# Image attention written as one stream of steps, with the expert weights split by GpSimd under it and the blank rows filled from GpSimd's queue in the token block

## The reference

```
# 1. image attention (L0)
hn = group_norm(x, 32 groups) * gamma + beta
q, k, v = conv1x1(hn, wq, bq), conv1x1(hn, wk, bk), conv1x1(hn, wv, bv)      # [b, 256, 1024]
attn = softmax(q^T k / sqrt(256), over keys)                                # [b, 1024, 1024]
x = x + conv1x1(v attn^T, wp, bp)
# 2. token block (L1_attn), t = tokens of x
u = layernorm(t);  h = rms_norm(u) * norm1_w
q, k = hyperbolic_linear(0.5 h onto the ball, q_w / k_w);  v = h v_w^T      # 8 heads of 32
a = softmax(-|q - k|^2 / sqrt(32), causal) v
y = u + a o_w^T;  h2 = rms_norm(y) * norm2_w
t = t + y + (silu(h2 gate_w^T) * (h2 up_w^T)) down_w^T
# 3. experts (L1_ffn): 8 experts, the top 2 for each token, hidden size 1024
t = t + sum_e comb[:, e] * (gelu(ln(t) w1[e]^T + b1[e]) w2[e]^T + b2[e])
```

## Time and profile before

| | |
|---|---|
| median of 3 runs | 1593.93 us (1593.6 to 1602.22) |
| profiled execution | 1580.31 us, of which the span is 1578.5 |
| busy: PE, DVE, ACT, POOL | 1219.1, 773.9, 708.9, 462.5 us |
| image attention | 26.9 to 336.2 us, PE busy for 246.0 |
| hand-over and first loads of the token block | 336.2 to 353.5 us, PE busy for 3.9 |
| token block up to its first scores | 353.5 to 420.4 us, PE busy for 27.3 |
| rest of the token block | 420.4 to 985 us, PE busy for 469.3 |
| routing, experts, output | 985 to 1578.5 us, PE busy for 465.7 |

### The profile page before, as it was taken

The page is one execution under the profiler, slowest core; times in us unless marked ns, Lnnn a source line. Parts: engine busy times, 40 slices in busy tenths (PEclk is TensorE's granted clock), DMA queues, the critical chain, the costliest instruction groups (busy, mean ns, idle before and its releaser), DMA issues. The chain is left out here.

```text
span 1578.5 us, 27016 instructions
## 1 busy us (share of the span) xinstructions
PE 1219.1 (77%) x8981; PEld 780.2 (49%) x8982; DVE 773.9 (49%) x1444; ACT 708.9 (45%) x1330; POOL 462.5 (29%) x403
## 2 busy tenths in 40 slices
PE   3888979546398789768977988532499999999992
PEld 1443434223134433333444334431388888888882
DVE  3855463405556564755466544643144444444441
ACT  3554352316566766766775663321133233333321
POOL 0000000010393059107800860177132233322331
PEclk9989999868699989998998999555799999999996
DMA  4486795950642084119403620999433333333326
GB/s 133 120 214 174 188 234 152 281 170 16 117 145 87 15 187 137 39 41 189 147 1 70 170 83 25 243 263 228 77 48 48 52 53 48 49 50 53 51 33 222
DMA packets 347541, 183.49 MB, mean 116 GB/s; under 512 B 271040, under 2 KB 333760, under 8 KB 347328
## 3 DMA queue, kind: packets, MB, share of 16 engines
q1 hardware_dynamic: 313920, 124.66, 34.2%
q0 software_dynamic: 25184, 56.64, 14.6%
q10 hardware_dynamic: 8352, 1.08, 0.5%
HBM read 38.66 MB, written 83.11 MB: 77 GB/s over the span
## 5 line engine op out<-in xcount | busy, mean ns | idle before, releaser
L2077 ACT ACTIVATE moe_hid<-moe_hbank,moe_b1T 128x256 f32<-128x256 f32 x312 | 130.4, 471 | 265.3 <-PE moe_hbank L2034 265.3
L2034 PE MATMUL moe_hbank<-moe_xT,l_w1T 128*128 128x256 f16 x1872 | 212.2, 274 | 42.9 <-DMA moe_xT<-rows_scratch 41.8
L2034 PEld LDWEIGHTS moe_hbank<-moe_xT,l_w1T 128*128 x1872 | 183.7, 98 | 65.2 <-issue 43.4
L2013 POOL DMA_INDIRECT acc_scratch<-moe_y,moe_meta x78 | 122.1, 1565 | 310.7 <-DVE moe_y L2104 288.1
L2049 PE MATMUL moe_ybank<-l_w2T,moe_hid_hi 128*128 x1248 | 206.4, 273 | 0.1
L1109 ACT ACTIVATE block_probs<-block_bank 128x1024 f32<-128x1024 f32 (+1 forms) x192 | 144.8, 809 | 76.6 <-PE block_bank L853 62.8
L2049 PE MATMUL moe_ybank<-l_w2T,moe_hid_lo 128*128 x624 | 170.1, 273 | 0.0
L2089 DVE TENSOR_SCALAR moe_hid_hi<-moe_hid 128x2048 f16<-128x2048 f32 x39 | 47.8, 1227 | 207.0 <-ACT moe_hid L2077 207.0
L2049 PEld LDWEIGHTS moe_ybank<-l_w2T,moe_hid_hi 128*128 128x128 f16 x1248 | 122.1, 98 | 14.6 <-issue 0.4
L850 PE MATMUL block_bank<-block_qkT 128*128 128x512 f16 (+3 forms) x384 | 95.9, 339 | 39.9 <-DMA block_qkT<-block_stack 28.8
L700 POOL COPY block_stack<-block_stack 128x512 f16<-128x512 f16 x16 | 11.2, 700 | 317.6 <-ACT block_stack L1093 317.6
(11 more groups left out here) (330 smaller groups left out, 2490.1 us busy)
## 6 DMA issues: line engine op xcount, KB each, us to landing
rows_scratch<-l_blank SPq DMA_DIRECT2D x32, 1056.0 KB, 5.7
block_raw<-in_L_ffn_w POOLq DMA_DIRECT2D x32, 512.0 KB, 4.6
w_parts<-block_raw_hi POOLq DMA_DIRECT2D x32, 256.0 KB, 4.4
w_parts<-block_raw_lo POOLq DMA_DIRECT2D x32, 256.0 KB, 4.7
l_xs<-in_x SPq DMA_DIRECT2D x8, 512.0 KB, 7.3
x_scratch<-l_xs SPq DMA_DIRECT2D x4, 1024.0 KB, 4.0
block_xin<-x_scratch SPq DMA_DIRECT2D x16, 256.0 KB, 4.4
acc_scratch<-block_res SPq DMA_DIRECT2D x16, 256.0 KB, 2.2
```

Of the source, the lines that this page charges most:

```text
L2013: pool.indirect_dma_start(acc, bass.IndirectOffsetOnAxis(ap=meta[r][:, t, 0:1].bitcast(U32), axis=0), y[r % 2][:, t, :], None, compute_op= ...
L2034: last = pe.matmul(hbank[:, c, :], w1T[:, e, wp, k, c * P:(c + 1) * P], xT[q][:, xp * CC + k, :], start=n == 0, stop=n == 5)
L2077: act.activation(hid[q][:, c, :], hbank[:, c, :], ACT.Gelu, bias=b1T[:, e, c:c + 1], scale=1.0 / (GAIN * GAIN)).then_inc(S["gelu_done"], 1)
```

## The change

The image attention becomes one list of 32 steps (`STEPS`), one for each tile of 128 queries. In step n TensorE makes the scores of tile n, then the weighted sum of tile n - 3 (`weighted`, `LAG` = 3), and then the share of the next image's 12 projection units that falls to this step: all 12 of image 1 in step 7, one or two in each step of images 1 and 2 (`share`). Queries, not channels, are now the output rows of the weighted sum: each has 24 matmuls 256 wide into one half of the bank `avx`. Two fp32 transposes put the tile's x into its other half. The probabilities are no longer divided by their row sum before they are split (scale `P_GAIN` instead of `rowinv`); `mix` does that on the output. `q` and `k` get two buffers each, the projections lose two of their four banks. SyncE stores half images as tokens.

GpSimd gets a list in this block: for each image two additions of `fold_bias` to `xs`, and 6, 6, 6 and 14 pieces of the expert weights. The block ends for GpSimd when all parts are stored.

The token block loads `t1` directly from `x1`, which now is [tokens x channels]; `x_turned`, `x_copy`, `xin` and their waits are gone. GpSimd's list there has the 34 fills, nine behind the four copies of each of the first three images and seven behind those of the last.

```diff
...
+                for n in range(STEPS):
+                    q = n % SLOTS
+                    if n >= SLOTS:
+                        sp.wait_ge(av_full, n - SLOTS + 1)
+                    sp.wait_ge(ph_hi_done, n + 1)
+                    sp.dma_start_transpose(pt_hi[q][:, :, :], ph_hi[q][:, :]).then_inc(turned[q], 16)
+                    sp.wait_ge(ph_lo_done, n + 1)
+                    sp.dma_start_transpose(pt_lo[q][:, :, :], ph_lo[q][:, :]).then_inc(turned[q], 16)
+                    if n >= 2 * HALF and n % HALF == 0:
+                        store(n // HALF - 2)
...
-                        for dst, src in fills[n::STEPS]:
-                            sp.dma_start(dst, src).then_inc(filled, 16)
...
+                def weighted(n):
+
+                    b, i, q = n // QB, n % QB, n % SLOTS
+                    if i == 0:
+                        pe.wait_ge(x_biased, CC * (b + 1))
+                        pe.wait_ge(unit_done, UNITS * (b + 1))
...
+                    if n >= 2:
+                        pe.wait_ge(mixed_done, n - 1)
...
+                    for c in range(CC):
+                        pe.transpose(avx[n % 2][:, 1, c * P:(c + 1) * P], xs[:, b, c, i * P:(i + 1) * P], ident[:, :])
+                    pe.wait_ge(turned[q], 32 * (n // SLOTS + 1))
+                    split_product(pe, avx[n % 2][:, 0, :], [(pt_hi[q][:, j, :], pt_lo[q][:, j, :], v_hi[b % 2][:, j, :], v_lo[b % 2][:, j, :])
+                                                            for j in range(QB)]).then_inc(av_full, 1)
...
+                    scores(b, i)
+                    if n >= LAG:
+                        weighted(n - LAG)
...
+                    for u in share(b, i):
+                        if u == 0:
+                            pe.wait_ge(hn_ready, (b + 2) * CC)
+                        unit(b + 1, u)
...
+            @block.gpsimd
...
+                load_piece(0)
+                load_piece(1)
                 for b in range(B):
...
+                    for c in range(CC):
+                        pool.wait_ge(hn_act, 2 * (b * CC + c) + 1)
+                        pool.tensor_scalar(xs[:, b, c, :], xs[:, b, c, :], fold_bias[:, c:c + 1], None, ALU.add).then_inc(x_biased, 1)
+                    for n in pieces_of(b):
+                        split_piece(n)
+                for q in range(2):
+                    pool.wait_ge(parts_stored[q], 16 * len(splits))
...
+                for n in range(STEPS):
+                    b, i = n // QB, n % QB
+                    row_max(b, i)
...
+                    if n >= LAG:
+                        weights_lo(n)
+                        inverse(n)
+                        residual(n - LAG)
...
+                for n, (dst, blank_row) in enumerate(fills):
+                    if n % (len(fills) // B + 1) == 0:
+                        second_high(n // (len(fills) // B + 1))
+                    pool.dma_start(dst, blank_row).then_inc(filled, 16)
+                pool.wait_ge(filled, 16 * len(fills))
...
                 def load(b, pr):
-                    if not isinstance(b, int) or b or pr > 1:
-                        sp.wait_ge(S["x_full"], b * PAIRS + (pr - 1))
-                    sp.dma_start(xin[pr % 2][:, :, :], x1[b].rearrange("(c p) (n q) -> n p c q", p=P, q=2 * P)[pr]).then_inc(S[f"xin{pr % 2}"], 16)
+                    sp.wait_ge(S["res_done"], b * PAIRS)
+                    sp.dma_start(t1[:, 2 * pr:2 * pr + 2, :], x1.rearrange("b (n t p) d -> b n p t d", p=P, t=2)[b, pr]).then_inc(S[f"x_loaded{pr}"], 16)
...
```

More of the change, by code:

```diff
@@ L279, with conv_attention @@
 PIECE = 1024
-def conv_attention(nc, xs, x1, scale, shift, norm, fills, w, bias, bias_loaded, fold_bias):
+def conv_attention(nc, xs, x1, scale, shift, norm, splits, raw_loaded, parts_stored, w, bias, bias_loaded, fold_bias, ident):
     SCALE = float(C) ** -0.5 / CW_GAIN ** 2
-    QKV, AV = 12, 4
+    UNITS, LAG = 12, 3
     SLOTS = 4
+    STEPS = B * QB
+    HALF = QB // 2
     with ExitStack() as ctx:
@@ L336, in _ @@
+                store(2 * B - 2)
+                store(2 * B - 1)
+                for half in stored:
+                    sp.wait_ge(half, 16 * B)
             @block.tensor
             def _(pe):
[L338 to L347, removed]
@@ new lines, in _ @@
+                pe.wait_ge(hn_ready, CC)
+                for u in range(UNITS):
+                    unit(0, u)
+                for n in range(STEPS):
[3 more added lines that the diff above has]
+                        weighted(n - LAG)
+                    if n == 2:
+                        pe.wait_ge(unit_done, UNITS)
+                        norm.average(pe, averages)
+                    for u in share(b, i):
+                        if u == 0:
+                            pe.wait_ge(hn_ready, (b + 2) * CC)
+                        unit(b + 1, u)
@@ L408, in _ @@
+                for n in range(STEPS - LAG, STEPS):
+                    weighted(n)
             @block.scalar
@@ new lines, in _ @@
+                for n in range(STEPS):
+                    b, i = n // QB, n % QB
+                    exps(b, i)
+                    if n >= LAG:
+                        mix(n - LAG)
+                    if n == 4:
+                        norm.root(act)
+                    if n == 5:
+                        act.wait_ge(norm.ready, 1)
+                        normalise(1)
+                    if n == 6:
+                        normalise(2)
+                    for u in share(b, i):
+                        high_part(b + 1, u)
+                    if n == QB + 2:
+                        normalise(3)
@@ L571, with token_block @@
 BARRIER = 4096.0
-def token_block(nc, x1, t2, ident, ident_h, weights, norm1_w, norm2_w, splits):
+def token_block(nc, x1, t2, ident, ident_h, weights, norm1_w, norm2_w, fills, filled):
     SCALE = 2.0 / (float(HD) ** 0.5 * QK_GAIN ** 2)
@@ L955, in first_front @@
                 def first_front():
-                    for pr in range(PAIRS):
-                        x_turned(0, pr)
                     for n in range(QKV_STRIPS):
@@ L2208, in build @@
         s = Scope(nc, whole, "all")
+        filled = s.sem("filled")
+        raw_loaded, parts_stored = ([s.sem(f"{n}{i}") for i in range(2)] for n in ("raw_loaded", "parts_stored"))
+        blank = s.sb("blank", [P, GT, ROW], F16)
+        make_blank_rows(nc, blank)
+        blocks_v = rows.rearrange("(n t p) r -> t p n r", p=P, t=GT)
+        fills = [(blocks_v[t][:, n:min(n + 8, BLOCKS), :],
+                  blank[:, t:t + 1, :].bitcast(U32).to_broadcast((P, min(8, BLOCKS - n), ROW // 2))) for n in range(0, BLOCKS, 8) for t in range(GT)]
         ident, ident_h = s.sb("ident", [P, P]), s.sb("ident_h", [P, P], F16)
```

398 lines of the change are left out of this document (159 added, 239 removed).

## The result

The changed kernel is slower: 1647.21 us (median of 4 runs, 1645.29 to 1650.8) against 1593.76 us for the kernel before (now the median of 4 runs), a ratio of 1.034 (95% interval 1.028 to 1.039). The prediction, 1578 us in 1562 to 1594, was wrong, and on the wrong side; rival C, at 0.12, had the place and the mechanism. The profiled execution has a span of 1643.5 us, 65.0 more than the one before.

The account below looks back on a forecast made before the run. The prediction saw late transposes behind the fills bounding the image attention (309.3 us, TensorE busy 246.0). Its terms, -9 - 2 - 6 + 1 = -16, took the median from 1593.9 to 1578 us, range 1562 to 1594.

Parts of the forecast that it names:

- rival C: Token block: fills starve the transposes, TensorE waits, +40 us or so, 1618 us; decides from a share under a third; chance 0.12.
- +1 us: Token block: cost of the 34 fills GpSimd issues there, their transfers sharing the queues with each pair's last transposes.
- half and half: Token block: fills and transposes share the queues equally, so image 0's eight remaining transposes need some 17 to 20 us.
- 21 of cover: Token block, image 0: time from the fills behind the fourth copy at 422 us until round 2 wants the transposes.
- Image attention, -9: Image attention: GpSimd sets its end, the token block starts at 331 instead of 339.9 us; bounds 318 and 340.
- The engines' chain: Image attention: TensorE, VectorE and ScalarE steps end at 289 us, about 305 with GpSimd meetings, at most 320.
- GpSimd's list: Image attention: 8 bias additions (22.3 us) and 32 pieces (259.8) from 28.1, last store at 310.3 us before meeting losses.
- the 12 allowed for meetings with VectorE: Image attention: GpSimd loses 12 us because its instructions and VectorE's two-input SBUF operations exclude each other.
- hand-over: End of the image attention: 7.8 us from the last store's issue to the next block's first load.
- Rival B: Image attention: GpSimd loses twice as much or the engines' chain outlasts it; stage ends at 340, 1587 us; chance 0.16.
- First loads of the token block, -2: Token block start: x arrives as tokens, so SyncE's hold of loads for TensorE's first eight transposes goes, -2 us.
- x transposes, -6: Token block: 16 fp32 transposes per following image leave TensorE, which has no gap there; 3 x 2 = -6 us.

Follow-up runs that it names:

- paced kernel: Changed kernel, but GpSimd issues an image's nine fills only when that image's last transposes have landed: 1562.46 us, ratio 0.990 to the kernel before.
- with 28 pieces: Changed kernel with fills waiting for the transposes, 28 of 32 pieces in the image attention, one per image in the token block: 1534.43 us, ratio 0.974.
- with 24: Changed kernel with fills waiting for the transposes, 24 of 32 pieces in the image attention, two per image in the token block: 1528.38 us, ratio 0.972.

## Why the prediction was wrong

**The step that failed is the price of the fills in the token block, "+1 us".** It shared the queues "half and half", so that eight transposes would be through in 17 to 20 us, just inside 21 of cover. The cover was right: from the fourth copy (586.62 in image 1) to TensorE running dry (618.84 - 11.40 = 607.4) is 20.8 us. The share was wrong. The queues alternate by packets, 250 bytes against 3972, and the fills of an image are 2448 packets. From the first fill to 457 us SyncE's queue, nearly all transposes, moves 6651, so the transposes outlast the fills and are through only when everything is. The term came out at 712.7 - 641.1 = 71.6 us, of which 64.6 stand in the four waits. The other 7 fit the clock: in the token block the same 3688 matmuls keep TensorE busy for 502.9 us in the changed kernel and for 493.4 in the paced one, at a mean granted clock of 0.87 and 0.92. The argument against C was that splitting's transfers had shared the queues without a wait. But those are one piece in 8.12 us; the fills are 9.7 MB at once.

**Rival C** named the place and decided at the right point ("a share under a third"; it was 87 of 661). It was too small, 20 and three times 10 where 24.0, 11.4, 22.0 and 7.2 came, and its own time of 1618 too low.

**Image attention, -9.** Measured -4.8. The engines' chain: VectorE's last residual ends at 295.3, against 289 without meetings and 305 with them. GpSimd's list: 310.3 + 12 = 322 was forecast for its last store, and it is issued at 320.5. The sum is near, but partly by luck: the subtraction took 2.30 us on average instead of 2.18, which is 4 us of the 12 allowed for meetings with VectorE, and another 3 are the additions of the bias, 25.7 us with their waits instead of 22.3. On VectorE `ph_lo` took 1.74 us on average instead of 1.28. What was mis-sized is the hand-over: 7.8 us was taken from a block whose last transfer was SyncE's, and behind GpSimd's it is 14.7 (320.47 to 335.17). Rival B did not happen: VectorE's last residual is 25 us ahead of GpSimd's last store, and with 28 pieces the token block starts at 303.5.

**First loads of the token block, -2.** From the first load to the first transposes was 67.6 us before and is 64.1 (65.5 in the paced kernel): -3.5 and -2.2. **x transposes, -6.** From the first transposes of image 0 to those of image 3 the paced kernel takes 441.2 us (400.03 to 841.18), the kernel before 444.1 (407.56 to 851.61): -2.9, half the forecast. Together, in the paced kernel, 641.1 against 647.8, -6.7 where the sum had -8.

**The sum.** -4.8 - 6.7 + 71.6 = 60.1; the rest of the 65.0 is the routing and expert part, 595.6 us instead of 590.8, which the change doesn't touch. In the paced kernel, where it is the same code, it took 585.3. With the fills behind the transposes the change gives 0.990, near the forecast, but partly by luck: in its trace -5.4 and -6.7 us stand where -9 and -8 were forecast, and 5.4 us come from the part that the change doesn't touch.

## What to carry to other kernels

When bulk transfers and small, urgent ones stand in different queues, count packets, not bytes: a large packet goes between any two small ones, so issue the bulk behind the landing of the urgent ones, by a wait on their semaphore (the token block then took 641.1 us with the same 34.9 MB and 639.6 without them). Before rewriting a stage, move what disturbs it: here that alone gave as much as the whole paced change. Work on an idle engine is free only at its hour: GpSimd's pieces cost 28 us when they slid later in the images, and 31 us as the last to end a block.

## What the runs showed of the hardware

- Two queues alternate packet for packet (1445 to 1476 in 17 us) though their packets differ 16 to 1 in size; with one packet of 3972 bytes between any two, the transposes went at 87 packets a us instead of 661.
- The exclusion between GpSimd and VectorE reaches operations with a single tensor input too: four [128 x 256] `TENSOR_SCALAR` took 4.42 us under pieces (796.84 to 801.26, beside a GpSimd scaling from 798.32 to 801.11), and 1.38 before at the same place. The Trainium skill (SBUF — State Buffer, section "Who interferes with whom") counts `tensor_scalar` in its two-port modes among the operations that can take the shared ports; the row agrees, though the trace does not show in which mode the instruction ran.
- GpSimd's queue can hold GpSimd. After six fills of image 1 the next issue waited 21.51 us, after three of image 3 12.48, while in images 0 and 2 nine went through in 8.0. Counted through the block, the stops come behind the 15th and the 30th fill (15 fills are 4080 packets), in both traces of the changed kernel and in the paced kernel alike, and each ends only when all fills issued before it have landed (1632 packets from 587 to 614 us, six fills of 272). With pieces between the fills there is no such stop. What sets the 15 was not tried.
- A block's end costs 4.1 us after the last bytes where GpSimd had done nothing for some time (for 11.6 us with 28 pieces, for 43 with 24), and 9.6 and 12.6 where it was the last to work.
